# VectorE forms the lower part of the next pair's A11 ahead of a tile's statistics, in the first phase of a graph-and-expert kernel

## What is computed

```
x = x + gnn(layernorm(x), edges, W, b)      # h = x @ W.T + b, then a sum over edges and self loops
x = x + ffn(layernorm(x), base_W, shared, routed, router)   # one dense product plus low-rank experts, 2 of 6
...
def _layernorm(x, axis=-1, eps=1e-05):
    m = jnp.mean(x, axis=axis, keepdims=True)
    v = jnp.var(x, axis=axis, keepdims=True)
    return (x - m) / jnp.sqrt(v + eps)
```

## Time and profile before

| what | value |
|---|---|
| median of 3 runs | 2082.25 us |
| the profiled execution's own time | 2083.08 us |
| its span | 2081.3 us |
| mean granted TensorE clock | 0.976 of full speed |
| TensorE matmul, weight load busy | 1957.5 us (94%), 1615.6 us (78%) |
| VectorE busy | 1470.2 us (71%) |
| ScalarE busy | 901.6 us (43%) |
| GpSimd busy | 922.2 us (44%) |

### The profile page before, as it was taken

The page is one execution under the profiler, slowest core; times in us unless marked ns, Lnnn a source line. Parts: engine busy times, 40 slices in busy tenths (PEclk is TensorE's granted clock), DMA queues, the critical chain, the costliest instruction groups (busy, mean ns, idle before and its releaser), DMA issues.

```text
span 2081.3 us, 31608 instructions
## 1 busy us (share of the span) xinstructions
PE 1957.5 (94%) x9583; PEld 1615.6 (78%) x9583; DVE 1470.2 (71%) x3525; ACT 901.6 (43%) x1533; POOL 922.2 (44%) x954
## 2 busy tenths in 40 slices
PE   7999999999999999934899999999999999999999
PEld 6777777777787777823788888888888888888887
DVE  6877887887876666644677767676767767676775
ACT  4455555555555545522333334333333333333332
POOL 1702444444424500025455555555555555555540
PEclk9999999999999999976999999999999999999999
DMA  6533554554443543482233333333333333333321
GB/s 248 203 115 138 177 185 153 179 183 152 177 142 133 145 152 148 147 269 58 83 91 89 96 98 98 90 100 102 97 85 90 100 84 100 101 99 86 90 68 51
DMA packets 148959, 260.20 MB, mean 125 GB/s; under 512 B 56077, under 2 KB 75357, under 8 KB 148822
## 3 DMA queue, kind: packets, MB, share of 16 engines
q1 hardware_dynamic: 99478, 237.85, 31.8%
q0 software_dynamic: 49344, 20.85, 7.9%
HBM read 273.80 MB, written 129.74 MB: 194 GB/s over the span
## 4 chain that ended last, share of the span: by engine, by line
issue 41%; PE 25%; POOL 23%; DVE 6%; ACT 2%; DMA 2%; POOLq 1%; DVEq 0%; ACTq 0%; SPq 0%
POOL acc L828 10%; PE bo L1489 5%; PE bo L1491 5%; PE bo L1493 5%; POOL piece L797 2%; POOL counted L764 2%; POOL counts L778 2%; POOL xpw L706 2%; POOL slots L785 2%; POOL pw L899 1%; DVE xn L1818 1%; POOL tick_pool L681 1%; PE bt L1539 1%; PE bo L1338 1%; PE bo L1340 1%
## 5 line engine op out<-in xcount | busy, mean ns | idle before, releaser
L828 POOL DMA_INDIRECT acc<-h_rows,row_now x312 | 499.5, 1601 | 113.2 <-issue 113.2
L1349 PE MATMUL bo<-wr_hi,left_hi 128*128 128x512 f32 x1008 | 403.1, 400 | 16.3 <-issue 10.1
L1353 PE MATMUL bo<-wr_hi,left_lo 128*128 128x512 f32 x1008 | 394.7, 392 | 0.0
L1351 PE MATMUL bo<-wr_lo,left_hi 128*128 128x512 f32 x1008 | 394.4, 391 | 0.0
L706 POOL TENSOR_TENSOR xpw<-xpin,neg_half 128x1 f32<-128x1 f32 x79 | 72.7, 920 | 504.2 <-DVE xpin L1660 504.2
L1489 PE MATMUL bo<-wr_hi,sum_hi 128*128 128x512 f32 x624 | 253.1, 406 | 0.0
L1493 PE MATMUL bo<-wr_hi,sum_lo 128*128 128x512 f32 x624 | 247.1, 396 | 0.0
L1491 PE MATMUL bo<-wr_lo,sum_hi 128*128 128x512 f32 x624 | 246.6, 395 | 0.0
L1349 PEld LDWEIGHTS bo<-wr_hi,left_hi 128*128 128x128 f32 x1008 | 190.3, 189 | 66.0 <-issue 29.6
L1353 PEld LDWEIGHTS bo<-wr_hi,left_lo 128*128 128x128 f32 x1008 | 190.1, 189 | 40.6
L1351 PEld LDWEIGHTS bo<-wr_lo,left_hi 128*128 128x128 f32 x1008 | 190.5, 189 | 36.4
(11 more groups left out here) (229 smaller groups left out, 4215.8 us busy)
## 6 DMA issues: line engine op xcount, KB each, us to landing
xn<-x SPq DMA_DIRECT2D x79, 512.0 KB, 4.4
r_rows<-xn SPq DMA_DIRECT2D x79, 512.0 KB, 2.7
acc<-r_rows SPq DMA_DIRECT2D x79, 512.0 KB, 4.3
out<-acc SPq DMA_DIRECT2D x79, 512.0 KB, 3.6
h_rows<-hrow SPq DMA_DIRECT2D x144, 256.0 KB, 2.2
acc<-h_rows,row_now POOLq DMA_INDIRECT x312
wr_raw<-w_t SPq DMA_DIRECT2D x16, 256.0 KB, 6.3
piece<-base_t SPq DMA_DIRECT2D x64, 64.0 KB, 4.2
```

What stands on the lines that cost most here:

```text
L828: nc.gpsimd.indirect_dma_start(to[:], None, h_dram, bass.IndirectOffsetOnAxis(ap=at, axis=0), bounds_check=NPAD - 1, oob_is_err=False, com ...
L1349: nc.tensor.matmul(ps, left_hi[n][:, k, :], wr_hi[n][:, k, :], start=False, stop=False, skip_group_check=True)
L1351: nc.tensor.matmul(ps, left_hi[n][:, k, :], wr_lo[n][:, k, :], start=False, stop=False, skip_group_check=True)
L1353: last = nc.tensor.matmul(ps, left_lo[n][:, k, :], wr_hi[n][:, k, :], start=False, stop=(k == 3), skip_group_check=True)
```

## The change

Two calls trade places in iterations p = 0 to 34. Nothing else moves; the instructions are the same.

```
                 if p + 1 < PAIRS:
+                    left_low(p + 1, A11, a11[:])
                     statistics(first(p + 1) + 1)
-                    left_low(p + 1, A11, a11[:])
                     scales(first(p + 1) + 1)
```

## The result

The changed kernel takes 2092.14 us, the median of 6 runs (2090.15 to 2095.29), against 2082.97 for the kernel before in 6 runs. The ratio is 1.0042, with a 95% interval of 1.0030 to 1.0054: 6 to 11 us slower. Forecast was 2089.3, or +7.1. The profiled execution has a span of 2088.4, 7.1 more than the 2081.3 of before.

A forecast was written before the change was run, and what follows sets the result against it. A loop through VectorE, GpSimd and ScalarE was taken to bound the kernel, with TensorE following. The terms 6.3 + 0.97 - 0.2 gave +7.1 us, on the median of 2082.25 a forecast of 2089.3, range 2080 to 2096.

The forecast's parts named there:

- Who leads: A loop through VectorE, GpSimd and ScalarE sets the pair's 21.6 us; TensorE follows with 0.8 us a pair to spare.
- Rival A: TensorE leads, so removing its stall at A11 is won: about 2068 us; chance 0.10.
- Term 1: The statistics on VectorE start later, behind the moved lower part of A11: +0.61 us a pair.
- Term 2: GpSimd's power, no longer under the lower part of A11, falls from 0.94 to 0.55: -0.40 us a pair.
- Rival C: GpSimd's power doesn't get shorter, so each pair pays 0.61: about 2102 us; chance 0.10.
- Term 3: Iterations 24, 27 and 28 absorb the delay, 34 feeds no further pair; 30 pairs pay 0.21: +6.3 us.
- Rival B: The loop's 0.21 disappears in a wait, only iteration 0 moves: within 1 us of 2083; chance 0.12.
- Term 4: In iteration 0 VectorE waits for A11's high part: un 1.65 later, less ScalarE's wait of 0.68: +0.97 us.
- Term 5: TensorE's A11 stall of 0.19 goes, T1's wait grows by about 0.4; only the last pair gains: -0.2 us.
- the last pair's 0.2: The last pair has no T1 behind it, so it keeps what A11's stall gave: -0.2 us.

## Why the prediction was right, point by point

**Who leads: right.** Four runs say so independently: 0.6 of VectorE's time is paid, 0.4 of TensorE's is not, and two cuts in the loop that leave TensorE's work alone are gained in full. Rival A (faster, about 2068) is out. It was not quite as simple as told, though: the loop has a companion through product A11, about 0.5 behind, which I did not list. The change makes the lower part of A11 earlier, so that loop got more slack and played no part.

**Term 1, +0.61: right.** 0.60 in the changed kernel (705.84 to 706.44), and +0.60 a pair in the run that makes it alone.

**Term 2, -0.40: right, 0.03 too large.** 0.37, for the power of 0.57 where I took 0.55 from the head. Rival C (the power stays long, about 2102) is out: all 35 powers of this place are at 0.55 to 0.58. The row on which it rested, the 0.92 at 964.33, has its reason on GpSimd itself. Its timeline in the kernel before:

```profile
963.95 0.75 POOL L823 CAST row_now<-offs 128x8 uint32<-128x8 int32 x1
964.33 0.92 POOL L899 TENSOR_TENSOR pw<-pin,neg_half 128x1 f32<-128x1 f32 x1
```

The cast ends at 964.70 and the power 0.55 behind it, at 965.25: a start in the record need not be the start of the work.

**Term 3, which pairs pay: right in kind.** Iterations 1 to 33 without three pay 6.85, 0.23 each on average; 24 and 27 pay 0.01 and -0.01, absorbed as told. Rival B, absorption everywhere, is out. Two iterations came out otherwise. Iteration 34, put at nothing, pays 0.22 up to the last lower part of A22. Iteration 28 did better than nothing, -0.61. In the kernel before, TensorE ran at the lower clock behind the long wait at T1 there, in the changed one it did not. The windows of before, then of after:

```profile
740.00:745.00 5.00, 5.00 (x21) 4.28 (x20) 4.96 (x7) 1.80 (x3) 0.00 (x0) 0.69 0.47 185
```

```profile
745.00:750.00 5.00, 2.56 (x16) 2.28 (x17) 3.39 (x5) 3.93 (x8) 0.00 (x0) 1.00 0.26 100
750.00:755.00 5.00, 5.00 (x24) 4.14 (x23) 4.12 (x10) 1.67 (x3) 0.55 (x1) 1.00 0.67 270
```

**Term 4, iteration 0, +0.97: right**, 0.92. The row shows VectorE waiting for the high part, as told:

```profile
127.38 0.69 DVE L1832 TENSOR_TENSOR left_lo<-a,left_hi 128x512 fp32r<-128x512 f32 x1 [1.37 <-ACT left_hi L1022]
```

**Term 5, TensorE: right in kind, not in its parts.** A11's stall was worth 0.27 and not 0.19, as I had left out that the second start behind it is late as well (0.31), and 0.18 of it went to A22 and not to T1, whose wait grew by 0.3 and not 0.4. As TensorE follows, none of this changes the time. What I did not tell either is that in the 16 pairs with weight pieces T2 waits for `un` (10.4 us in the waits above), as TensorE comes there earlier than `un` does. It costs nothing, since T1 waits anyway.

**The sum: close, in part by luck.** At the last lower part of A22 the changed kernel is 8.57 later (893.64 against 885.07): 1.19 of it are there before the first pair, in code that the change does not touch, and the pairs make 7.4, where the terms, without the last pair's 0.2, made 7.3. That these agree to 0.1 is partly luck: the 30 pairs and iteration 34 paid 0.8 more than I had put down, and iteration 28 gave 0.6 back.

The last pair's -0.2 did not show. Its last two products begin behind a wait for ScalarE in both kernels (2.61 before, 3.26 in the changed one), and they begin 8.88 later (908.14 against 899.26). In the kernel before TensorE then ran a part of them at its lower clock, in the changed one not, and the last matmul is only 7.32 later (913.48 against 906.16). The windows of before, then of after:

```profile
900.00:905.00 5.00, 5.00 (x16) 3.95 (x15) 2.67 (x5) 2.56 (x5) 1.02 (x2) 0.66 0.76 198
```

```profile
908.00:913.00 5.00, 4.86 (x21) 4.05 (x22) 3.46 (x6) 2.88 (x5) 1.70 (x2) 1.00 0.50 142
```

So the 7.1 by which the span is longer holds +1.2 from ahead of the first pair and -1.6 from the clock, for which I had no term, and its match with the forecast to a tenth is luck. The firm part is the 0.23 a pair. The medians differ by 9.2, with an interval of 6 to 11 that holds the 7.1; the profiled execution of the changed kernel is the fastest of its six, 2.0 below their median.

## What to carry to other kernels

An instruction put into the wait for another engine is free only if it leaves that engine alone: here 0.68 us of VectorE in the shade of a GpSimd power cost 0.37, which it took from the power. Before a stall on the busiest engine is removed, compare the period with what that engine takes when it is late (20.8 against 21.6): if it has room, the stall only moves to its next wait. And look at the loops that are second, too; a step that has half a microsecond of slack leads as soon as it is moved by one.

## What the runs showed of the hardware

A GpSimd power on 128x1 takes 0.55 to 0.58 us by itself. With a VectorE instruction over it that reads two tensors in SBUF it does not get slower by a factor, it ends about 0.4 after that instruction has ended: by 0.40 to 0.45 in all 73 powers at L706 of the kernel before that took over 0.7 us. Two lengths show it:

```profile
97.08 1.27 DVE L1712 SCALAR_TENSOR_TENSOR hrow<-b_rows,dis,hrow 128x1024 f32<-128x1024 f32 x1
...
97.24 1.51 POOL L706 TENSOR_TENSOR xpw<-xpin,neg_half 128x1 f32<-128x1 f32 x1 [3.00 <-DVE xpin L1660]
```

Here VectorE ends at 98.35 and the power at 98.75; with the lower part of A11 it is 700.72 and 701.15. With one of the two inputs of the same lower part read from PSUM the power takes 0.57. The GPSIMD Engine Reference of the Trainium skill, section Key points, names this contention for VectorE instructions with two SBUF inputs. The traces agree, and add the size: here the tiny instruction did not end before the large one was through, at all 70 powers from the first pair on. Freeing both of a pair's powers was worth 23.5 us (2081.78 to 2058.28).
